# Pairs of images in the front of a deformable-convolution kernel, and GpSimd on part of the sampling tensors

## The chip, the cores and the metric

The kernel runs on one core of a Trainium2 chip. The metric is the device time of one execution in microseconds. The engines of the core run side by side and meet only at semaphores: TensorE (PE; its weight loads are PEld), VectorE (DVE), ScalarE (ACT), GpSimd (POOL) and SyncE (SP), which here only issues transfers. Each engine takes its own instructions in the order in which they are written.

## What is computed

The input x has 4 images of 64 channels and 16 x 16 pixels. Two blocks follow each other, cut here to what matters:

```
x = x + dcn(norm_over_channels(x))
    om      = conv3x3(x, w_off) + b_off          # 27 channels: 9 y offsets, 9 x offsets, 9 masks
    ys, xs  = pixel + tap + offset               # fractional places, one for each of 9 taps
    sampled = bilinear(x, ys, xs) * sigmoid(mask)
    out     = sum over taps and channels of sampled * w_dcn
t = t + moe(norm_over_channels(t))               # tokens = 1024 pixels, 64 channels
    the two best of 8 experts, softmax of the two logits
    out     = sum over experts of weight * (gelu(t W1 + b1) W2 + b2)
```

## The kernel before

**Sampling as a product.** A bilinear sample is a sum over all 256 source pixels with the weight hat(ys - y) * hat(xs - x), where hat(d) = max(0, 1 - |d|). The kernel makes this matrix of weights for each tap (256 source by 256 target pixels) and multiplies the image by it on TensorE. The matrix is made in two ways. Images 0 and 1 are DIRECT: the hats of the y and of the x axis are made with the target pixel on the partition, 16 numbers each, and a product of the two, repeated along the two axes (`pr`, line 589, 512 columns for a chunk of two taps and half of the pixels), gives the transposed matrix; TensorE transposes it (T steps, line 861), ScalarE or VectorE copies it out of PSUM (E steps, lines 480 and 739), and M steps (line 875) multiply the image. Images 2 and 3 are SPREAD: their hats are made with (tap, place) on the partition (`hrow`, and `hlast` for the ninth tap), written to a tensor in DRAM, and read back so that they lie spread over the source pixels (30 reads of SyncE, lines 332 and 335); a product (`pd`, line 600) gives the matrix with no transpose.

**The front, step by step.** For each image: `stats`, `rstd` (a power on GpSimd, line 349) and `xn` (line 699) normalize; `xnT` transposes; `xpl` (ScalarE) and `xpu` (VectorE, line 705) write two halves of a padded image; `conv` (line 830) makes the 27 offset channels in four column groups of 32 partitions, each a partial sum; `om` copies them. DIRECT: `omT` transposes and sums the groups, `pos`, `dist` (line 566), `abs` (ScalarE), `relu` (line 724), `haty` (line 577) make the hats, then 10 products `pr` for each image, written as pr image.chunk.half. SPREAD: R steps (lines 848 to 852) pick the rows by a matmul with a 0/1 matrix, whose last rows add the place constants, and ScalarE takes absolute values or the tanh of the mask; `hr` steps of VectorE (lines 609 to 618) finish. The constants of the R steps are rows made by GpSimd on one partition (`make_rows`) and brought to their places by seven small transfers of SyncE (lines 310 to 317).

**The rest.** C steps (line 886) project by `w_dcn`; `xr` adds; `oT`, `st`, `rstdt`, `lna`, `xT`, `xs` normalize again; gate, `top`, `idx`, `wd` choose experts for a half (two images) at a time; H (line 937), Gelu (`g`, line 511), O (line 948), `tmp` (line 770) are the experts, `ya` (GpSimd, line 416) and F add them up.

**The order** of each engine is a list of steps written out by hand at lines 44 to 67, and HOMES and PAIR_HOMES give each step its PSUM bank. A step waits only for the semaphores of what it reads and of what it overwrites. The products write to a ring of AT_RING = 3 chunks, so chunk u waits until chunk u - 3 is transposed.

Of the kernel before, what the change touches and what calls it, by code (L numbers as in the profile page):

```python
# [33 lines left out]
DIRECT, SPREAD = (0, 1), (2, 3)  # L34
# [5 lines left out]
POS_ROW = 3 * OMG + OM  # L40
LESS = 2 * HW
BIG = LESS + 3 * TAPS * W

PE_ORDER = (
    "xnT0 early4 conv0 xnT2 xnT3 omT0 xnT1 conv2 conv3 conv1 R2.0 R2.1 R3.1 T0.0 T0.2 T0.3 R3.0 T0.1 T0.4 omT1 T0.5 T0.8 T0.7 "
    "T0.6 M0.0 M0.4 M0.1 M0.3 M0.2 T1.0 T1.1 T1.3 T1.5 T1.2 T1.4 T1.7 T1.6 T1.8 M1.0 M1.3 M1.2 M1.4 M1.1 C0.0 C1.0 C0.1 C1.1 M2.2 "
    "oT1 oT0 M2.0 M2.3 M2.1 M2.4 xT0 xT1 C2.0 M3.0 M3.1 C2.1 gate0 H0.2.0 H0.0.0 H0.1.1 H0.1.0 H0.0.1 H0.2.1 oT2 M3.3 M3.2 wdT0 "
    "M3.4 C3.0 O0.1 C3.1 sp0.0 sp0.1 H0.3.0 oT3 O0.0 O0.2 xT2 xT3 H0.3.1 gate1 H1.0.0 H1.0.1 H1.1.0 H1.1.1 H1.2.1 wdT1 O0.3 O1.0 "
    "sp1.0 sp1.1 H1.3.1 H1.2.0 H1.3.0 O1.1 O1.2 O1.3.0 F0 O1.3.1 Fa1.0 Fa1.1 F1.0 F1.1 "
).split()  # L50
ACT_ORDER = (
    "xpl0 om0 xpl2 xpl3 xpl1 tanhm0 abs0 om2 selr0 om3 ay2 al2 tm2 tl2 om1 E0.0 tm3 E0.3 ay3 E0.1 E0.2 tanhm1 E0.5 abs1 E0.7 E0.6 "
    "se0.0 al3 E0.4 se0.3 E1.0 E1.1 tl3 E1.5 E1.2 se0.1 E1.7 E1.4 E1.8 se1.2 se0.4 se1.1 se1.3 se2.2 se2.3 se2.1 xs1 xs0 se2.4 "
    "g0.2.0.1 tanhd0 se3.1 g0.0.0.0 g0.2.0.0 g0.0.0.1 g0.1.0.0 g0.1.0.1 g0.1.1.0 g0.1.1.1 g0.2.1.0 se3.3 g0.0.1.1 g0.0.1.0 se3.4 "
    "wts0 g0.2.1.1 ss0.1 g0.3.0.1 g0.3.0.0 xs2 xs3 g0.3.1.1 g0.3.1.0 g1.0.0.1 g1.0.0.0 g1.0.1.1 tanhd1 g1.0.1.0 g1.1.1.0 g1.1.0.1 "
    "g1.1.0.0 g1.1.1.1 g1.2.1.1 wts1 g1.2.1.0 ss1.0 ss1.1 g1.2.0.0 g1.2.0.1 g1.3.1.0 g1.3.0.0 g1.3.0.1 g1.3.1.1 "
).split()
DVE_ORDER = (
    "stats0 stats1 xn0 base0 xpu0 xn2 xn3 xn1 xpu2 xpu3 pos0 dist0 xpu1 relu0 haty0 pr0.1.0 pr0.0.0 pr0.0.1 pr0.1.1 hr2.0 hr2.1 "
    "hr2.2 pr0.2.0 pr0.2.1 pr0.4.0 pr0.4.1 pr0.3.0 pr0.3.1 pos1 dist1 E0.8 relu1 haty1 pr1.2.1 pr1.0.0 pr1.0.1 pr1.1.0 hr3.0 "  # L60
# [19 lines left out]
        "conv2 R2.0 T0.0 T0.1 T0.8 M0.4 C0.0 oT0 M3.4 O0.1 F0 Fa1.1 "  # L80
    ),
    (
        "T0.2 T0.7 M0.1 M1.0 M1.4 M2.0 xT2 O1.1 "
    ),
    (
        "R3.0 T0.5 M0.0 M0.3 T1.0 T1.2 T1.8 xT3 "
# [929 lines left out]
```

## Time and profile before

| | us |
|---|---|
| median of 3 runs | 90.9 (90.84 to 90.98) |
| the profiled execution | 90.21 |
| its span, first to last instruction | 88.4 |
| TensorE busy | 80.9 |
| VectorE busy | 64.5 |
| ScalarE busy | 46.9 |
| GpSimd busy | 20.6 |

The span leaves out 1.8 us around it. A row of a timeline gives start, length, engine, line, operation, output and inputs with their sizes, and in brackets how long the engine stood idle before it and who released it. One matrix product in float32 is two matmul instructions. In a row of several instructions the length runs from the first start to the last end. Lengths on GpSimd are rough.

### The profile page before, as it was taken

What the parts mean: (1) busy time and instruction counts of PE and PEld (TensorE: products, weight loads), DVE (VectorE), ACT (ScalarE), POOL (GpSimd) and SP (SyncE); (2) the same over time, 40 slices, a digit from 0 to 9 for tenths busy, and PEclk for the clock granted to TensorE, in tenths of its full rate; (3) what the DMA queues carried; (4) which work ended last, traced back from release to release, by engine and by line L of the source; (5) the groups of instructions that cost most, each with busy time, mean ns of one, the idle gap of its engine ahead of it and who ended that gap; (6) DMA issues with size and microseconds to landing.
All of it is one profiled execution on the core that took longest, in us unless ns stands there. A gap on an engine that the chain in (4) does not pass through costs nothing.

```text
span 88.4 us, 1853 instructions
## 1 busy us (share of the span) xinstructions
PE 80.9 (92%) x606; PEld 48.7 (55%) x606; DVE 64.5 (73%) x199; ACT 46.9 (53%) x95; POOL 20.6 (23%) x39
## 2 busy tenths in 40 slices
PE   3986799999999999969969999999999999999970
PEld 3974455499657968846646535734345332433540
DVE  5999989998999999999954998519667613213470
ACT  4110565787956843211410899814439986889000
POOL 7499820000003040005000002200309103200720
DMA  1520049340999997089999500000000000000012
GB/s 32 160 61 2 2 77 399 129 124 15 293 259 319 296 314 259 1 222 272 311 320 320 164 4 0 7 0 0 0 0 0 0 0 0 0 7 0 0 59 59
DMA packets 7192, 9.92 MB, mean 112 GB/s; under 512 B 1690, under 2 KB 3648, under 8 KB 7184
## 3 DMA queue, kind: packets, MB, share of 16 engines
q1 hardware_dynamic: 6848, 9.42, 35.9%
q0 software_dynamic: 192, 0.30, 1.0%
q8 instruction: 5, 0.08, 0.4%
q10 hardware_dynamic: 144, 0.10, 0.3%
q14 instruction: 3, 0.02, 0.1%
HBM read 8.95 MB, written 0.85 MB: 111 GB/s over the span
## 4 chain that ended last, share of the span: by engine, by line
PE 56%; DVE 19%; DMA 11%; issue 5%; SPq 3%; ACT 1%; POOL 1%; DVEq 0%
PE banks L937 17%; PE banks L948 15%; DMA hat_rows<-hlast 6%; DMA spread_hats<-hat_rows 6%; PE banks L861 5%; DVE front L589 4%; PE banks L875 4%; PE banks L830 3%; DVE xn L699 2%; PE banks L848 2%; SPq L335 2%; PE banks L928 1%; PE banks L886 1%; DVE spread_hats L600 1%; PE banks L919 1%
## 5 line engine op out<-in xcount | busy, mean ns | idle before, releaser
L511 ACT ACTIVATE front<-banks,b_col 128x512 f32<-128x512 f32 x32 | 19.8, 700 | 8.7 <-PE banks L937 5.4
L937 PE MATMUL banks<-x2s,w_sb 64*128 64x512 f32 x64 | 15.2, 608 | 0.0
L948 PE MATMUL banks<-front,w_sb 128*64 128x512 f32 (+1 forms) x72 | 14.7, 549 | 0.0
L770 DVE SCALAR_TENSOR_TENSOR spread_hats<-banks,b_col,spread 128x512 f32<-128x512 f32 (+1 forms) x9 | 6.1, 689 | 9.9 <-PE banks L948 7.3
L349 POOL TENSOR_TENSOR rs<-ve,power 128x2 f32<-128x2 f32 (+1 forms) x6 | 5.2, 868 | 28.7 <-DVE ve L639 27.5
L589 DVE TENSOR_TENSOR front<-hats 128x512 f32<-128x512 f32 (+1 forms) x20 | 11.5, 630 | 0.5 <-PE banks L861 0.3
L600 DVE TENSOR_TENSOR spread_hats<-spread_hats 128x1024 f32<-128x1024 f32 (+1 forms) x10 | 10.8, 1107 | 0.7 <-DMA spread_hats<-hat_rows 0.6
L483 ACT ACTIVATE smp<-banks 128x256 f32<-128x256 f32 x14 | 5.2, 389 | 9.5 <-PE banks L875 9.5
L875 PE MATMUL banks<-spread_hats,xn 128*64 128x256 f32 x72 | 9.0, 384 | 0.7 <-DVE spread_hats L600 0.7
L937 PEld LDWEIGHTS banks<-x2s,w_sb 64*128 64x128 f32 x64 | 5.7, 186 | 6.4 <-issue 2.5
L948 PEld LDWEIGHTS banks<-front,w_sb 128*64 128x64 f32 x72 | 4.9, 137 | 7.8 <-issue 6.2
L861 PE MATMUL banks<-ident,front 128*128 128x128 f32 x72 | 9.1, 277 | 0.1
L480 ACT ACTIVATE front<-banks 128x512 f32<-128x512 f32 x15 | 8.2, 592 | 1.7 <-PE banks L861 1.7
L861 PEld LDWEIGHTS banks<-ident,front 128*128 128x128 f32 x72 | 7.9, 142 | 1.4 <-DVE front L589 0.5
L875 PE MATMUL banks<-front,xn 128*64 128x256 f32 x72 | 8.3, 383 | 0.0
L875 PEld LDWEIGHTS banks<-spread_hats,xn 128*64 128x64 f32 x72 | 4.8, 136 | 3.2 <-issue 1.1
L875 PEld LDWEIGHTS banks<-front,xn 128*64 128x64 f32 x72 | 5.1, 136 | 2.6 <-ACT front L480 0.6
L802 PE MATMUL banks<-ident 128*128 128x128 f32 x26 | 5.1, 374 | 1.4 <-POOL power L356 1.4
L289 POOL DMA_DIRECT2D hat_rows<-hrow x2 | 1.4, 708 | 18.5 <-DVE hrow L609 15.8
L802 PEld LDWEIGHTS banks<-ident 128*128 128x128 f32 x26 | 4.8, 286 | 1.4 <-POOL power L356 1.4
L886 PE MATMUL banks<-smp,wdcn 128*64 128x128 f32 x80 | 5.5, 275 | 0.1
L886 PEld LDWEIGHTS banks<-smp,wdcn 128*64 128x64 f32 x80 | 4.7, 137 | 1.3 <-issue 0.7
(117 smaller groups left out, 102.0 us busy)
## 6 DMA issues: line engine op xcount, KB each, us to landing
spread_hats<-hat_rows SPq DMA_DIRECT2D x24, 256.0 KB, 5.0
w_sb<-in_w SPq DMA_DIRECT2D x2, 512.0 KB, 4.6
spread_hats<-hat_rows SPq DMA_DIRECT2D x6, 128.0 KB, 5.6
xc<-in_x_ch SPq DMA_DIRECT2D x1, 256.0 KB, 5.5
hat_rows<-hrow SPq DMA_DIRECT2D x2, 128.0 KB
hat_rows<-hrow POOLq DMA_DIRECT2D x2, 128.0 KB, 5.5
xt<-in_x_tok SPq DMA_DIRECT2D x1, 192.0 KB, 2.5
wdcn<-in_w_dcn SPq DMA_DIRECT2D x1, 160.0 KB, 2.9
```

The costliest lines, as they stand in the source:

```text
L349: pool.tensor_tensor(dst, src, power[:, 0:src.shape[1]], ALU.pow).then_inc(ready, 1)
L480: act.activation(a_sb[:, k, :, :].rearrange("p s t -> p (s t)"), bank(f"T{d}.{k}"), ACT.Copy).then_inc(tap_saved["ACT"], 1)
L511: act.activation(hid[:, m % H_RING, half, c, :], two_banks(f"H{h}.{j}.{c}")[:, half * 512:(half + 1) * 512], ACT.Gelu, bias=b1_col[:, col: ...
L589: dve.tensor_tensor(at[:, u % AT_RING, j, 0:m, :].rearrange("p k (y x) -> p k y x", x=W), hats[:, i, j, k0:k0 + m, :].unsqueeze(3).broadca ...
L600: dve.tensor_tensor(spread_hats[:, i, 1:, k0:k0 + m, :], spread_hats[:, i, 1:, k0:k0 + m, :], spread_hats[:, i, 0, k0:k0 + m, :].unsqueeze ...
L770: dve.scalar_tensor_tensor(part(tmp[:, h, j, :]), part(bank(step_o)[:, :]), b2_col[:, j:j + 1], part(spread[:, h, j, :]), ALU.add, ALU.mul ...
L802: pe.matmul(home[:, 0:P], ident[:, :], ident[:, :], start=True, stop=True)
L861: last = pe.transpose(bank(step)[:, st * HW + j * P:st * HW + (j + 1) * P], at[:, u % AT_RING, j, place, st * P:(st + 1) * P], ident[:, :])
L875: last = pe.matmul(bank(step)[col * C:(col + 1) * C, 0:HW], xn[:, NT * b + st, 0, :], tap(b, k, st), start=(st == 0 or len(taps) == 1), st ...
L886: last = pe.matmul(bank(f"C{b}.0")[j * O:(j + 1) * O, 0:P], wdcn[:, q, :], smp[:, b, q, j * P:(j + 1) * P], start=(q == 0), stop=(q == CHU ...
L937: last = pe.matmul(two_banks(step)[:, half * 512:(half + 1) * 512], w1_sb[rows_, j, c * P:(c + 1) * P], x2s[rows_, 2 * h:2 * h + 2, :], st ...
L948: last = pe.matmul(part(bank(step)[O * half:O * half + O, :]), w2_sb[:, j + PAIRS * half, c, :], part(hid[:, (PAIRS * h + j) % H_RING, hal ...
```

## The change

DIRECT and SPREAD stay as they are. What changes:

- **Pairs in the front.** `xnT`, `xpl`, `xpu`, `conv` and `om` take two images at once: images 0 and 1, then 2 and 3. A pair's convolution uses the four column groups as two images by two partial sums. `omT`, `pos` and `tanhm` come once, for both DIRECT images. The first transfer of `xt` brings four tiles instead of two. `xpu1` is ScalarE's, `om1` is VectorE's.
- **Row products.** R1.2 (the last tap of both images), R1.0 and R1.1, in which a product uses only one image's 64 rows. Seven products where there were eight. The pixel places are added by `om1`, from a tensor `pos_rows` that GpSimd makes (`make_places`), and the tap's shift is a bias of ScalarE's absolute value (`make_shifts` on GpSimd). `hat_of` is 512 wide, `place_of` (512 wide) is new, `pick` is made in four steps instead of one. `make_rows` and its seven transfers are gone, `hlast` holds both images. All writes of hat rows are SyncE's, both images' ahead of the first reads.
- **GpSimd** makes `dist1`, nine of the twenty `pr` products (seven of 512 columns, two of 256) and `pd2.0` and `pd2.3` of the ten spread products. `sel0` comes later.
- `relu1` moves to ScalarE, `xs2` to VectorE, `ss0.0` to ScalarE, and E and se steps are shared out anew. All orders and bank homes are new.

```diff
 POOL_ORDER = (
-    "rstd0 rows0 rstd1 sel0 dw3 rstdt0 rstdt1 rstdt2 rstdt3 ya0.1 ya0.2 ya0.3 ya1.1 ya1.2 "
+    "rstd0 rstd1 place0 shift0 dist1 pr0.1.1 pr0.2.1 pr0.4.0 pr0.3.1 pr1.0.0 pr1.1.1 pr1.2.1 pr1.3.1 pr1.4.0 pd2.0 pd2.3 rstdt0 "
+    "rstdt1 sel0 rstdt2 rstdt3 ya0.1 ya0.2 ya0.3 ya1.1 ya1.2 "
 ).split()
 PE_ORDER = (
-    "xnT0 early4 conv0 xnT2 xnT3 omT0 xnT1 conv2 conv3 conv1 R2.0 R2.1 R3.1 T0.0 T0.2 T0.3 R3.0 T0.1 T0.4 omT1 T0.5 T0.8 T0.7 "
-    "T0.6 M0.0 M0.4 M0.1 M0.3 M0.2 T1.0 T1.1 T1.3 T1.5 T1.2 T1.4 T1.7 T1.6 T1.8 M1.0 M1.3 M1.2 M1.4 M1.1 C0.0 C1.0 C0.1 C1.1 M2.2 "
...
+    "xnT0 early4 xnT1 conv0 omT0 conv1 R1.2 R1.0 R1.1 T0.2 T0.3 T0.0 T0.1 T0.4 T0.5 M0.0 T0.6 T0.7 T0.8 M0.1 M0.2 M0.3 T1.0 T1.1 "
+    "T1.5 T1.3 T1.2 T1.4 T1.7 T1.6 T1.8 M0.4 M1.2 M1.0 M1.1 M1.3 C0.0 M1.4 C0.1 C1.0 oT0 C1.1 M2.0 oT1 M2.2 M2.1 M2.3 M2.4 xT0 "
...
 DVE_ORDER = (
-    "stats0 stats1 xn0 base0 xpu0 xn2 xn3 xn1 xpu2 xpu3 pos0 dist0 xpu1 relu0 haty0 pr0.1.0 pr0.0.0 pr0.0.1 pr0.1.1 hr2.0 hr2.1 "
-    "hr2.2 pr0.2.0 pr0.2.1 pr0.4.0 pr0.4.1 pr0.3.0 pr0.3.1 pos1 dist1 E0.8 relu1 haty1 pr1.2.1 pr1.0.0 pr1.0.1 pr1.1.0 hr3.0 "
-    "pr1.1.1 pr1.2.0 pr1.3.0 pr1.3.1 pr1.4.1 pr1.4.0 hr3.1 hr3.2 E1.6 E1.3 se0.2 se1.0 pd2.0 pd2.2 se1.4 pd2.1 pd2.3 xr0 xr1 "
...
+    "stats0 stats1 xn0 xn1 xn3 xn2 xpu0 base0 pos0 dist0 om1 relu0 haty0 pr0.0.0 pr0.1.0 pr0.0.1 hy2 hx2 pr0.2.0 hm2 hl1 hy3 "
+    "pr0.3.0 hx3 hm3 haty1 pr0.4.1 E0.5 pr1.2.0 E0.6 pr1.0.1 pr1.1.0 pr1.3.0 E1.3 pr1.4.1 E1.4 E1.1 se0.4 se1.2 pd2.1 se1.0 E1.8 "
+    "pd2.2 xr0 se1.4 xr1 st0 st1 pd2.4 lna0 lna1 pd3.0 se2.4 xr2 se3.0 top0 st2 pd3.2 pd3.1 pd3.3 se3.2 pd3.4 se3.3 idx0 wd0 xr3 "
...
+        def product(engine, b, q, j):
+            i = DIRECT.index(b)
+            u = CHUNKS * i + q
+            k0, m = chunk_taps(q)[0], len(chunk_taps(q))
+            engine.wait_ge(*saved(haty_ready, f"haty{b}"))
+            if u >= AT_RING:
+                before, chunk = divmod(u - AT_RING, CHUNKS)
+                engine.wait_ge(tap_T, upto(*(f"T{DIRECT[before]}.{k}" for k in chunk_taps(chunk))))
+            shape = [P, m, H, W]
+            engine.tensor_tensor(
+                at[:, u % AT_RING, j, 0:m, :].rearrange("p k (y x) -> p k y x", x=W),
+                hats[:, i, j, k0:k0 + m, :].unsqueeze(3).broadcast_to(shape),
+                hats[:, i, j, TAPS + k0:TAPS + k0 + m, :].unsqueeze(2).broadcast_to(shape),
+                ALU.mult).then_inc(*one_more(at_ready, f"pr{b}.{q}.{j}"))
...
                 elif kind == "conv":
                     take_bank(step, saved(om_saved, f"om{b}"))
...
+                    for t in range(2 * KS):
+                        kx, ky = divmod(t, KS)
+                        for i in range(2):
+                            q = 2 * i + t % 2
+                            last = pe.matmul(bank(step)[q * OMG:(q + 1) * OMG, 0:HW], woff[:, t, :],
+                                             xpad[:, 2 * b + i, ky:ky + H, 2 * kx:2 * kx + W], start=(t < 2), stop=(t >= 2 * KS - 2))
...
+                        for c in ((0, 1) if n[1] == 0 else (2,)):
+                            for i in range(2):
+                                rows_ = slice(i * IMG_ROWS, (i + 1) * IMG_ROWS)
+                                first = i * 512 + c % 2 * HW
+                                last = pe.matmul(two_banks(step)[:, first:first + HW], pick[rows_, c * P:(c + 1) * P], om_sp[rows_, :],
+                                                 start=True, stop=True)
```

## Rows read from the trace of the kernel before

**Rows 1.** The page: busy us, share of the span, and instructions of each engine.

```profile
PE 80.9 (92%) x606; PEld 48.7 (55%) x606; DVE 64.5 (73%) x199; ACT 46.9 (53%) x95; POOL 20.6 (23%) x39
```

**Rows 2.** Busy times by stretch: length, busy of each engine, clock, DMA share.

```profile
17.10:31.00 13.90, 13.84 (x117) 11.37 (x116) 13.09 (x28) 10.63 (x24) 0.91 (x2) 1.00 0.73 209
31.00:37.60 6.60, 6.52 (x80) 5.09 (x80) 6.60 (x10) 2.19 (x6) 1.04 (x2) 1.00 0.61 189
```

**Rows 3.** The timeline of TensorE, 11 to 47 us: start, length, line, operation.

```profile
11.16 2.78 PE L830 MATMUL banks<-xpad,woff 128*32 128x256 f32 x36
...
17.12 1.53 PE L861 MATMUL banks<-ident,front 128*128 128x128 f32 x12
18.49 1.03 PE L848 MATMUL banks<-big 128*128 128x256 f32 x4
...
20.23 0.53 PE L838 MATMUL banks<-omsum,om_sb 128*128 128x32 f32 x4
...
26.53 4.60 PE L861 MATMUL banks<-ident,front 128*128 128x128 f32 x36
31.06 4.16 PE L875 MATMUL banks<-front,xn 128*64 128x256 f32 x36
...
37.50 1.06 PE L875 MATMUL banks<-spread_hats,xn 128*64 128x256 f32 x8
39.24 0.43 PE L895 MATMUL banks<-ident,xc 64*128 64x64 f32 x4 [0.68 <-DVE xc L628]
...
46.18 1.08 PE L875 MATMUL banks<-spread_hats,xn 128*64 128x256 f32 x8 [0.70 <-DVE spread_hats L600]
```

**Rows 4.** The start: GpSimd's line 359, VectorE's timeline and its line 699 (min/median/max).

```profile
L359 POOL IOTA hat_of<- x1: 594/594/594, 1.5 to 1.5; 128x384 f32 x1
...
3.75 0.85 DVE L539 BATCH_NORM_STATS2 st<-xt 128x6 f32<-128x64 f32 x6
...
L699 DVE TENSOR_SCALAR xn<-xt,mv,rs x8: 333/390/722, 5.3 to 9.9; 128x128 f32<-128x128 f32 x8
...
7.46 0.43 DVE L705 COPY xpad<-banks 64x256 f32<-64x256 f32 x1
```

**Rows 5.** The timeline of VectorE, 11 to 44 us.

```profile
11.34 0.85 DVE L566 TENSOR_TENSOR dist<-pos,grid 128x576 f32<-128x576 f32 x1
...
23.21 0.46 DVE L724 TENSOR_SCALAR hats<-dist 128x576 f32<-128x576 f32 x1
...
24.20 2.50 DVE L589 TENSOR_TENSOR front<-hats 128x512 f32<-128x512 f32 x4
26.62 0.42 DVE L609 TENSOR_SCALAR hrow<-hrow 128x512 f32<-128x512 f32 x1
...
42.96 1.21 DVE L600 TENSOR_TENSOR spread_hats<-spread_hats 128x1024 f32<-128x1024 f32 x1
```

**Rows 6.** GpSimd and VectorE at once: lines 349, 660 (ns, min/median/max) and both timelines.

```profile
L349 POOL TENSOR_TENSOR rs<-ve,power x6: 696/713/1322, 4.0 to 62.0; 128x2 f32<-128x2 f32 x5, 128x6 f32<-128x6 f32 x1
L660 DVE CAST topf<-topi x2: 171/494/816, 49.9 to 68.1; 128x8 f32<-128x8 uint32 x2
...
54.69 1.07 POOL L349 TENSOR_TENSOR rs<-ve,power 128x2 f32<-128x2 f32 x1 [12.47 <-DVE ve L639]
54.52 0.68 DVE L600 TENSOR_TENSOR spread_hats<-spread_hats 128x512 f32<-128x512 f32 x1
...
67.62 1.26 POOL L416 TENSOR_TENSOR ya<-ya,spread_hats 128x512 f32<-128x512 f32 x1
68.10 0.82 DVE L660 CAST topf<-topi 128x8 f32<-128x8 uint32 x1
```

**Rows 7.** SyncE's queue: the first and the last issues of image 2's 15 reads.

```profile
20.66 0.62 SPq L332 DMA_DIRECT2D spread_hats<-hat_rows  x1
...
29.03 1.32 SPq L335 DMA_DIRECT2D spread_hats<-hat_rows  x2
```

**Rows 8.** The page: DMA issues with KB each and us to landing.

```profile
spread_hats<-hat_rows SPq DMA_DIRECT2D x24, 256.0 KB, 5.0
```

## What the change will do: the prediction

> **What bounds the kernel now.** I read the page first: TensorE is busy for 80.9 of 88.4 us, VectorE for 64.5, GpSimd for 20.6 [rows 1]. Then the busy times by stage: from 17.1 to 31.0 TensorE is busy 13.84 of 13.90 us and VectorE 13.09, and from 31.0 to 37.6 they are busy 6.52 and all 6.60 of 6.60 us [rows 2]. So the front has two bounds that touch: TensorE never rests, and VectorE, which makes what TensorE transposes, hardly does. GpSimd is free there. The clock of TensorE is granted in full in all of it. Then TensorE's timeline [rows 3]: the offset convolutions and the row products (R steps) lie ahead of the first transposes (T steps) at 17.12, the last T step ends at 26.53 + 4.60 = 31.13, and later there are two pauses, 0.68 us for VectorE's add and 0.70 us for a spread product. I take two marks from this, **the start of the T steps (17.12)** and **their end (31.13)**. What comes behind the second mark is TensorE work in a fixed order that the change leaves nearly as it is.
>
> **What the pairs take from TensorE.** Three images' convolutions take 2.78 us [rows 3], 6 waves of four column groups with the second half empty, so 0.46 each; a pair of images fills 3 waves where two images took 4, so two waves (0.9 us) fall away. R steps: R3.0, two products of 256 columns (4 matmul instructions), takes 1.03 us [rows 3]; four such steps, 8 products, are about 4.1 us. After: one product, and 6 that lie on half of the rows each, two at a time, 4 waves of about 0.5 us. That takes 2.1 us away, or 0.5 if halves don't run together. The omT steps become one, 0.36 us less (estimate from 0.53 for 4 matmuls [rows 3]). Only what now lies inside 17.12 to 31.13 counts: R3.0 and omT1, about 0.9 + 0.36 = 1.25 us; the rest empties time in which TensorE will wait for the first products anyhow. Against it, one tap product, M0.4, moves behind the last T step: 0.46 us, a ninth of 4.16 [rows 3].
>
> **What it does to the start.** GpSimd makes more index tensors, 384 wide ones for 0.59 [rows 4], so VectorE gets the fourth at about 3.2 and needs 1.3 for the four steps on `pick` and 0.35 for zeroing the padding: 4.85. Four tiles of statistics, from 0.85 us for six and as much again with their aggregates: 1.0, 5.85. The power of four columns, between 0.70 (two) and 1.32 (six) [rows 4, 6]: 1.0, 6.85. Four xn tiles at 0.35 [rows 4]: 8.25; two images more, which stand ahead of the copy, 1.4, and the copy of a pair 0.7 (0.43 was one image [rows 4]): 10.4. conv0 3 waves: 11.85; its copy, omT0 and `pos`: 12.85; `dist0` 0.8 [rows 5]: 13.65; its absolute value on ScalarE 0.7; `relu0` 0.46 [rows 5]: **14.9**, and without anything in the way products would begin at 15.4, against 13.93 before. Bounds: 14.0 if the index tensors hide, 16 if `xn` is slowed by GpSimd's place tensors, as tiles now range from 333 to 722 ns [rows 4]. The constant rows no longer go through seven small DMAs on SyncE's queue, so the weights are issued some 4 us earlier; nobody waited for them.
>
> **What it moves from VectorE to GpSimd,** the step that decides. A two-input operation of 512 columns takes GpSimd 1.26 us [rows 6] and VectorE 2.50 / 4 = 0.62 [rows 5]. Until the last T step GpSimd has `dist1` (576 columns, 1.4), 7 products of 512 (8.9) and 2 of 256 (about 0.65 each, 1.3): 11.6 us. VectorE keeps 9 products (5.6), 2 halves (0.7), two `haty` (0.9, each taken as a `relu`, 0.46), four row clips at 0.28 (half of the columns of a step of 0.42, with its fixed part; 1.1), two masks of rows (0.7) and the last row (0.7, both estimates from the same 0.42): 9.7 us [rows 5]. If both ran side by side, this would be over in 11.6 us.
>
> Do they? The only rows in which they meet say no. The cast of the indices takes 171 ns alone and 816 ns beside a GpSimd sum: it begins at 68.10 and ends at 68.92, when the sum (67.62 + 1.26 = 68.88) does [rows 6]. A power takes GpSimd about 0.70 us, and 1.07 when it starts at 54.69, under a spread product of VectorE that ends at 55.20: it ends 0.56 us behind that [rows 6]. In both, the later one waits for the earlier, and only its start-up (0.1 us on VectorE, 0.14 on GpSimd) is hidden. Products and `hats` steps on VectorE have their inputs in SBUF, as this spread product has; copies out of PSUM (E, se) have not. I take it that the two streams go **one behind the other**: 9.7 + 11.6 = 21.3 us, less the hidden start-ups, 0.14 for ten GpSimd operations and 0.07 for some ten of VectorE, 2.1 us: 19.2. From 14.9 that ends at 34.1; the last T step, half a microsecond, at 34.6. Nothing is left idle for it to hide in: no GpSimd product can start on image 1 before `haty1`, and VectorE reaches that only behind the rows.
>
> The Trainium skill speaks of this case (SBUF — State Buffer, "Who interferes with whom"): a VectorE instruction with two SBUF inputs and a GpSimd instruction that reads SBUF exclude each other, the second blocking fully until the first is done. The trace agrees in the two meetings above. By its rule with nothing hidden the streams would take the whole 21.3 us, and the forecast would be 2.1 us higher.
>
> **The sum,** against the profiled execution (span 88.4 us, 90.21 in all, so 1.8 around it, and 0.7 under the median 90.9): T steps end 34.6 - 31.13 = +3.5; M0.4 behind them +0.5; of the two pauses of 1.4 us half goes (products are on GpSimd's account there, and image 3's rows are read at once behind image 2's) -0.7; `fin0` no longer stands ahead of the last products, -0.2, and ScalarE instead of VectorE copies `ss0.0`, +0.2; small waits from the new orders in the second half +0.2, an estimate. +3.5: **94.4** for the median 90.9 (a span of about 92).
>
> Covers that I count on: the 30 reads of spread hats now follow each other without a stop, 19.4 us of SyncE's queue (image 2's 15 take 20.66 to 30.35 [rows 7]). With the masks and `hlast` done near 27 and their writes issued by 28, they end near 47.5, and the last lands 5.0 us later [rows 8], near 52.5; its product ran at 54.52 before [rows 6] and is wanted near 58 then. If the cover is gone, each microsecond of it is one. `pd2.0` and `pd2.3` on GpSimd cost 2.4 us each (the double of 1.21 [rows 5]); they follow its last product at 34.1 and are there at about 37 and 40.5 (between VectorE's `pd2.1` and `pd2.2`). TensorE needs 6.4 us of its own between its last T step and the first spread samples, as now (31.13 to 37.50 [rows 3]): they are wanted near 41.5 and 43, and behind them waits the first `rstdt`, which the layer norm needs at about 43.5. That cover is thin: 1 to 2 us.
>
> **Rivals.**
> A, the forecast: one behind the other with start-ups hidden, 94.4 (93 to 95.8). Chance 0.48.
> B, the same, dearer: nothing hidden (+2.1, 96.5), or GpSimd's products cost more than its plain sum, as their inputs are repeated along two axes and the sum's are not (a fifth more on 9 of them is 2 us), or `rstdt` comes late: 95.8 to 98.5. For it: `xn` tiles of up to 722 ns beside GpSimd. Chance 0.24.
> C, on the other side: the two engines run side by side, since only the cast's kind of operation excludes GpSimd. The place that decides is the first pair of products. GpSimd has `dist1` until 16.35, then `pr0.1.1` until 17.65: T steps begin at 17.7 (+0.6). From there TensorE is fed (VectorE and GpSimd make a chunk in 1.3 us, TensorE uses it in 1.9) and has 1.25 less: -0.65 at the second mark with M0.4 inside this sum, and both pauses go, -1.4: -2.0, 88.9 (88.2 to 90.6). It decides from the point at which overlap recovers over 3.5 us of the 9.7. For it: `pr` is not the cast; against it the power beside the spread product. Chance 0.21.
> D: exclusion is real but TensorE's order fills the holes with M steps, 90.7 to 93. Chance 0.07, mostly slower.
>
> **How the numbers follow.** The likeliest gives 94.4. The range of 80% spans C's middle to B's: 88.8 to 97.8. 0.2% (about 0.2 us) is about what a measurement of this kernel can tell from no change. Faster: C but for its edge, 0.20; within: 0.03; slower: A, B and most of D, 0.77.
>
> **What would show it.** In A, VectorE's products beside GpSimd's take 1.2 to 1.9 us each, GpSimd's more than 1.3, their ends alternating; TensorE is idle 4 to 6 us between its first T step and about 35, its transposes waiting for `front`; the last T step ends at 34 to 36. In C VectorE's products stay at 0.68 and the last T step ends before 31. Convolutions of a pair near 1.4 us and four R waves near 2 show the first part. I am wrong in mechanism if products keep their lengths, and wrong in size if the start-ups hide more, if the first product doesn't begin near 17, or if a wait behind 38 (for `pd2.0`, `pd2.3`, `rstdt0`) becomes the longest.

## The result, and the profile after

The changed kernel takes **94.8 us** (94.56 to 96.03 in 4 executions); the kernel before took 90.87 beside it (90.23 to 90.98). The ratio is 1.044, interval 1.038 to 1.050. The profiled execution took 94.73 with a span of 92.9 us, 4.5 more than the 88.4 of before. In what follows, a ratio is that of each kernel's fast executions, those within 1.5% of its fastest, while a median is of all of them, and of "pairs only", "late start" and "no products" the profiled execution was a slow one, so that little behind the T steps is read from it.

The page of after, then its busy times in one stretch (length, busy of TensorE, its weight loads, VectorE, ScalarE and GpSimd with instructions, TensorE's granted clock, DMA share, GB/s):

```profile
PE 81.3 (88%) x600; PEld 49.1 (53%) x600; DVE 61.1 (66%) x193; ACT 45.3 (49%) x87; POOL 45.1 (49%) x60
...
PEclk9997599996599999999999999999999999999999
...
L381 POOL TENSOR_TENSOR front<-hats 128x512 f32<-128x512 f32 (+1 forms) x9 | 12.8, 1435 | 4.4 <-PE banks L944 4.4
...
L381 DVE TENSOR_TENSOR front<-hats 128x512 f32<-128x512 f32 (+1 forms) x11 | 10.6, 982 | 3.0 <-PE banks L944 3.0
```

```profile
19.00:31.00 12.00, 9.32 (x63) 7.18 (x65) 9.89 (x18) 7.34 (x18) 9.57 (x7) 0.86 0.38 116
```

GpSimd's busy time doubled and more (20.6 to 45.1), VectorE's fell only by 3.4, and TensorE has as much to do as before, 81.3 us [rows 1]. Where TensorE had no idle time [rows 2], it is idle for 2.7 of 12 us. And the clock line shows something that the forecast doesn't have: it falls twice, in the slices from 7 to 11.6 and from 21 to 25.5 us.

TensorE's timeline of after (start, length, line, operation, count, idle time ahead and what ended it):

```profile
7.94 1.20 PE L896 MATMUL banks<-ident,xn 128*128 128x128 f32 x4 [2.70 <-DVE xn L765]
8.93 1.91 PE L877 MATMUL banks<-ident 128*128 128x128 f32 x8
10.64 1.02 PE L896 MATMUL banks<-ident,xn 128*128 128x128 f32 x4
11.59 1.50 PE L908 MATMUL banks<-xpad,woff 128*32 128x256 f32 x24
...
16.45 0.67 PE L924 MATMUL banks<-om_sp,pick 128*128 128x256 f32 x2 [0.70 <-DVE om_sp L776]
17.05 1.57 PE L934 MATMUL banks<-om_sp,pick 64*128 64x256 f32 x12
20.62 4.71 PE L944 MATMUL banks<-ident,front 128*128 128x128 f32 x24 [2.00 <-DVE front L381]
...
27.19 1.50 PE L944 MATMUL banks<-ident,front 128*128 128x128 f32 x12 [0.84 <-POOL front L381]
...
31.77 4.45 PE L944 MATMUL banks<-ident,front 128*128 128x128 f32 x36
...
50.99 1.11 PE L1020 MATMUL banks<-x2s,w_sb 64*128 64x512 f32 x4
```

L944 is the line of the T steps. They begin at 20.62 instead of 17.12 and end at 31.77 + 4.45 = **36.22** instead of 31.13 [rows 3]: +5.1. The first 24 of them take 4.71 us, 0.196 each, where the last 36 take 0.124 each. From the second mark to the end of the span it is 56.7 us, against 57.3. So the loss lies wholly ahead of the second mark; behind it the change wins 0.6. The two pauses of before, 0.68 and 0.70 us [rows 3], are gone.

VectorE's timeline of after:

```profile
14.35 0.27 DVE L785 TENSOR_TENSOR pos<-banks,base 128x108 f32<-128x108 f32 x1 [2.05 <-PE banks L916]
14.66 0.76 DVE L360 TENSOR_TENSOR dist<-pos,grid 128x576 f32<-128x576 f32 x1
...
16.22 0.45 DVE L790 TENSOR_SCALAR hats<-dist 128x576 f32<-128x576 f32 x1
16.70 0.46 DVE L369 SCALAR_TENSOR_TENSOR hats<-tanh_m,hats 128x288 f32<-128x288 f32 x1
17.20 1.54 DVE L381 TENSOR_TENSOR front<-hats 128x512 f32<-128x512 f32 x1
18.66 1.54 DVE L381 TENSOR_TENSOR front<-hats 128x512 f32<-128x512 f32 x1
```

And GpSimd's:

```profile
18.14 1.50 POOL L381 TENSOR_TENSOR front<-hats 128x512 f32<-128x512 f32 x1
19.61 1.50 POOL L381 TENSOR_TENSOR front<-hats 128x512 f32<-128x512 f32 x1
...
23.83 3.21 POOL L381 TENSOR_TENSOR front<-hats 128x512 f32<-128x512 f32 x1 [1.28 <-PE banks L944]
...
28.40 1.06 POOL L381 TENSOR_TENSOR front<-hats 128x512 f32<-128x512 f32 x1 [0.34 <-PE banks L944]
...
35.30 2.36 POOL L391 TENSOR_TENSOR spread_hats<-spread_hats 128x1024 f32<-128x1024 f32 x1
```

While both engines make products, one of VectorE's begins every 1.46 us (17.20, 18.66) and one of GpSimd's every 1.47 (18.14, 19.61). Alone, GpSimd's takes 1.06 and VectorE's 0.62 [rows 5]: 1.68 for one behind the other, 0.2 hidden. That is the forecast's picture, but it doesn't fill the stretch: of VectorE's nine products of 512 columns only four take over 1.2 us, and by the page's lines of the products (L381) GpSimd's wait 4.4 us for transposes and VectorE's 3.0, since a product needs a free place in the ring. The product at 23.83 is a case of its own: 3.21 us, during which VectorE ran one step behind another, and it ended only when VectorE had turned to a copy out of PSUM.

### The profile page after: what moved, and what is told of

It reads as the page before. It is cut to its first block, busy times and chain, and to the rows that moved or that the text cites. A ratio compares the mean times of both kernels' runs of the same rounds, so it can differ in the third digit from the quotient of the medians.

```text
span 92.9 us, 1837 instructions
## 1 busy us (share of the span) xinstructions
PE 81.3 (88%) x600; PEld 49.1 (53%) x600; DVE 61.1 (66%) x193; ACT 45.3 (49%) x87; POOL 45.1 (49%) x60
## 4 chain that ended last, share of the span: by engine, by line
PE 76%; DVE 10%; POOL 7%; issue 3%; ACT 0%; POOLq 0%; DVEq 0%
PE banks L1020 16%; PE banks L1031 15%; PE banks L958 15%; PE banks L944 10%; PE banks L969 5%; POOL front L381 3%; DVE front L381 3%; PE banks L908 3%; PE banks L896 2%; PE banks L877 2%; PE banks L1011 1%; PE banks L984 1%; PE banks L1002 1%; POOL rs L416 1%; PE banks L994 1%
## 5 line engine op out<-in xcount | busy, mean ns | idle before, releaser
L381 POOL TENSOR_TENSOR front<-hats 128x512 f32<-128x512 f32 (+1 forms) x9 | 12.8, 1435 | 4.4 <-PE banks L944 4.4
L416 POOL TENSOR_TENSOR rs<-ve,power 128x2 f32<-128x2 f32 (+1 forms) x6 | 6.2, 1036 | 17.9 <-DVE ve L709 15.1
L1031 PE MATMUL banks<-front,w_sb 128*64 128x512 f32 (+1 forms) x72 | 14.8, 550 | 0.0
L944 PE MATMUL banks<-ident,front 128*128 128x128 f32 x72 | 10.6, 308 | 3.0 <-DVE front L381 2.0
L381 DVE TENSOR_TENSOR front<-hats 128x512 f32<-128x512 f32 (+1 forms) x11 | 10.6, 982 | 3.0 <-PE banks L944 3.0
L944 PEld LDWEIGHTS banks<-ident,front 128*128 128x128 f32 x72 | 9.3, 159 | 4.7 <-issue 4.0
L600 ACT ACTIVATE front<-banks 128x512 f32<-128x512 f32 x12 | 6.6, 599 | 5.8 <-PE banks L944 5.8
L391 DVE TENSOR_TENSOR spread_hats<-spread_hats 128x1024 f32<-128x1024 f32 (+1 forms) x8 | 9.0, 1141 | 0.0
L603 ACT ACTIVATE smp<-banks 128x256 f32<-128x256 f32 x12 | 4.2, 386 | 9.7 <-PE banks L958 9.7
L517 POOL TENSOR_TENSOR ya<-ya,spread_hats 128x512 f32<-128x512 f32 x3 | 3.8, 1269 | 7.6 <-DVE spread_hats L845 7.4
L391 POOL TENSOR_TENSOR spread_hats<-spread_hats 128x1024 f32<-128x1024 f32 x2 | 5.1, 2540 | 3.2 <-DMA spread_hats<-hat_rows 3.2
L517 POOL TENSOR_TENSOR ya<-spread_hats 128x512 f32<-128x512 f32 x2 | 2.5, 1272 | 7.6 <-DVE spread_hats L845 7.6
```

The source lines that it names most:

```text
L381: engine.tensor_tensor(at[:, u % AT_RING, j, 0:m, :].rearrange("p k (y x) -> p k y x", x=W), hats[:, i, j, k0:k0 + m, :].unsqueeze(3).broa ...
L391: engine.tensor_tensor(spread_hats[:, i, 1:, k0:k0 + m, :], spread_hats[:, i, 1:, k0:k0 + m, :], spread_hats[:, i, 0, k0:k0 + m, :].unsque ...
L416: pool.tensor_tensor(dst, src, power[:, 0:src.shape[1]], ALU.pow).then_inc(ready, 1)
L517: pool.tensor_tensor(ya[:, h, :], so_far, tmp[:, h, j, :], ALU.add).then_inc(ya_ready, 1)
L600: act.activation(a_sb[:, k, :, :].rearrange("p s t -> p (s t)"), bank(f"T{d}.{k}"), ACT.Copy).then_inc(tap_saved["ACT"], 1)
L944: last = pe.transpose(bank(step)[:, st * HW + j * P:st * HW + (j + 1) * P], at[:, u % AT_RING, j, place, st * P:(st + 1) * P], ident[:, :])
```

## The experiments

The forecast stands, but a sum can be right by luck. Two causes can be told apart, since each can be had alone: **the pairs** and **GpSimd's share**. "The pairs" stands here for all of the change but GpSimd's share, with the row products and the moved steps; these weren't separated further. One measure serves in all runs: the time at which the first product begins, and the end of the T steps. The table collects them from the timelines of VectorE and TensorE (profiled executions), with the median time and its ratio to the kernel before on the same chip.

| kernel | first product | T steps begin | T steps end | end less first product | median us | ratio (interval) |
|---|---|---|---|---|---|---|
| before | 13.93 | 17.12 | 31.13 | 17.2 | 90.87 | 1 |
| after | 17.20 | 20.62 | 36.22 | 19.0 | 94.8 | 1.044 (1.038 to 1.050) |
| pairs only | 18.40 | 19.84 | 35.78 | 17.4 | 95.76 | 1.053 (1.040 to 1.065) |
| GpSimd only | 14.01 | 17.77 | 33.18 | 19.2 | 93.29 | 1.028 (1.018 to 1.038) |
| after, warm | 16.20 | 19.59 | 33.99 | 17.8 | 93.85 | 1.030 (1.015 to 1.046) |
| pairs only, warm | 16.18 | 19.42 | 33.58 | 17.4 | 94.20 | 1.038 (1.028 to 1.048) |
| middle filler | 18.45 | 21.71 | 36.11 | 17.7 | 94.80 | 1.040 (1.030 to 1.051) |
| early start | 16.00 | 20.22 | 33.83 | 17.8 | 93.72 | 1.034 (1.028 to 1.040) |
| rows first | 16.00 | 19.31 | 33.77 | 17.8 | 93.59 | 1.029 (1.018 to 1.040) |
| distances only | 16.00 | 19.10 | 33.53 | 17.5 | 94.26 | 1.035 (1.024 to 1.046) |
| late start | 16.82 | 18.87 | 33.62 | 16.8 | 96.12 (lowest 94.08) | – |

The fifth column is what the study came to. With pairs it is 17.4 to 17.8, whoever makes the products and whatever the orders are, but for after itself (19.0, with slow transposes in it).

The lines behind the first and third columns, of before, of "pairs only, warm" and of "late start":

```profile
13.93 2.50 DVE L589 TENSOR_TENSOR front<-hats 128x512 f32<-128x512 f32 x4
```

```profile
30.29 3.29 PE L944 MATMUL banks<-ident,front 128*128 128x128 f32 x28 [0.30 <-DVE front L381]
```

```profile
16.82 2.50 DVE L590 TENSOR_TENSOR front<-hats 128x512 f32<-128x512 f32 x4
...
29.02 4.60 PE L866 MATMUL banks<-ident,front 128*128 128x128 f32 x36
```

**Pairs only.** After, with `dist1`, all products and all spread products back on VectorE; ScalarE takes image 1's absolute value later, as `dist1` comes later.

```diff
-    "rstd0 rstd1 place0 shift0 dist1 pr0.1.1 pr0.2.1 pr0.4.0 pr0.3.1 pr1.0.0 pr1.1.1 pr1.2.1 pr1.3.1 pr1.4.0 pd2.0 pd2.3 rstdt0 "
-    "rstdt1 sel0 rstdt2 rstdt3 ya0.1 ya0.2 ya0.3 ya1.1 ya1.2 "
+    "rstd0 rstd1 place0 shift0 rstdt0 rstdt1 sel0 rstdt2 rstdt3 ya0.1 ya0.2 ya0.3 ya1.1 ya1.2 "
```

> The changed kernel with dist1, the nine products and pd2.0 and pd2.3 back on VectorE (abs1 and relu1 stand later on ScalarE so that nothing blocks); all else of the change stays. Theory 1 (VectorE's two-input operations and GpSimd's exclude each other, so GpSimd takes more from the front than it gives): products on VectorE back at 0.68 us each, last transposes end near 33 instead of 36.2, 90 to 92 us. Theory 2 (the pairs are what costs, GpSimd helps): VectorE has 9 more products and is later, 96 us or more.

Measured 95.76, above theory 1 and just below theory 2. If GpSimd's share were the cause, this would have been the good kernel; it is no better than after. Its products take 0.68 us as expected, but the T steps end at 35.78, not near 33. TensorE shows why the first product comes as late as 18.40: the 24 convolution instructions of the first pair need 2.65 us, where the next 24 need 1.50.

```profile
7.93 1.20 PE L896 MATMUL banks<-ident,xn 128*128 128x128 f32 x4 [2.29 <-DVE xn L765]
...
11.62 2.65 PE L908 MATMUL banks<-xpad,woff 128*32 128x256 f32 x24
...
15.44 1.50 PE L908 MATMUL banks<-xpad,woff 128*32 128x256 f32 x24
```

**GpSimd only.** The kernel before with the same steps on GpSimd (`dist1`, nine products, two spread products). GpSimd now comes late to image 3's rows, so SyncE writes them.

```diff
-    "rstd0 rows0 rstd1 sel0 dw3 rstdt0 rstdt1 rstdt2 rstdt3 ya0.1 ya0.2 ya0.3 ya1.1 ya1.2 "
+    "rstd0 rows0 rstd1 sel0 pr0.1.1 pr0.2.1 pr0.4.0 pr0.3.1 dist1 pr1.0.0 pr1.1.1 pr1.2.1 pr1.3.1 pr1.4.0 pd2.0 pd2.3 rstdt0 "
+    "rstdt1 rstdt2 rstdt3 ya0.1 ya0.2 ya0.3 ya1.1 ya1.2 "
```

> The kernel before with GpSimd alone: it makes dist1, the same nine products, pd2.0 and pd2.3, and SyncE writes image 3's hat rows in its place; no pairs. Theory 1: VectorE's products take 1.0 to 1.5 us beside GpSimd's, TensorE idles 2 us or more before 35, 93 to 96 us. Theory 2 (side by side): products stay at 0.68 us and the time is 89 to 91 us.

Measured 93.29, ratio 1.028, so some 2.5 us over the before of its chip. Here GpSimd's share does cost: the T steps start 0.65 late, with a pause of 0.50 for a product, and end 2.05 late, at 30.02 + 3.16 = 33.18; behind them stands a second price. GpSimd's spread product (start 31.87, 2.53 us) holds VectorE's small mask step, and TensorE waits for the copy behind that:

```profile
32.12 2.57 DVE L621 SCALAR_TENSOR_TENSOR hrow<-mrow,hrow 128x256 f32<-128x256 f32 x1
```

```profile
36.08 3.24 PE L883 MATMUL banks<-front,xn 128*64 128x256 f32 x28 [1.88 <-DVE front L747]
```

The same step for the other image took 0.43 in this trace. In the changed kernel the row masks stand ahead of GpSimd's last products, and none meets `pd2.0`.

**After, warm, and pairs only, warm.** Both get more filler for TensorE: 18 in place of 9 transposes of the identity before the first `xn`, and eight more groups of two ahead of the T steps. No result depends on them; what they change is that TensorE isn't idle there.

```diff
-WARM = 9
+WARM = 18
...
-    "xnT0 early4 xnT1 conv0 omT0 conv1 R1.2 R1.0 R1.1 T0.2 T0.3 T0.0 T0.1 T0.4 T0.5 M0.0 T0.6 T0.7 T0.8 M0.1 M0.2 M0.3 T1.0 T1.1 "
+    "xnT0 early4 xnT1 conv0 omT0 conv1 R1.2 R1.0 R1.1 early8 T0.2 T0.3 T0.0 T0.1 T0.4 T0.5 M0.0 T0.6 T0.7 T0.8 M0.1 M0.2 M0.3 "
```

> The changed kernel with dummy matmuls in its two early pauses of TensorE: 18 instead of 9 at the very start, and 8 between R1.1 and T0.2. Theory 3 (the lower clock of the transposes after the pause of 2 us is on the path, since both engines wait for transposes to free the ring): granted clock 1.00 throughout, transposes at 0.13 us an instruction, 1.5 to 2.5 us less, 92.3 to 93.3 us. Theory 4 (the products set the pace, the clock is beside it): the clock comes back and the time stays within 0.5 us of 94.8.

> Pairs without GpSimd, and with the dummy matmuls. Theory 1 with theory 3: 88.5 to 90.5 us, faster than both kernels. Theory 1 alone: as the kernel with pairs only. Theory 2: 95 us.

Measured 93.85 (93.76, 93.94, 93.23 and 95.19) and 94.20 (94.19 to 94.22); after gains 1.0 us by the fillers, where theory 3 had 1.5 to 2.5. TensorE's timeline of "after, warm":

```profile
9.78 0.66 PE L896 MATMUL banks<-ident,xn 128*128 128x128 f32 x4
10.59 1.50 PE L908 MATMUL banks<-xpad,woff 128*32 128x256 f32 x24 [0.16 <-DVE xpad L771]
...
29.54 4.45 PE L944 MATMUL banks<-ident,front 128*128 128x128 f32 x36
```

VectorE's products in it (count, min/median/max in ns, start of the first and of the last):

```profile
L381 DVE TENSOR_TENSOR front<-hats x11: 414/693/1680, 16.2 to 32.1; 128x512 f32<-128x512 f32 x9, 128x256 f32<-128x256 f32 x2
```

and the same row of "pairs only, warm":

```profile
L381 DVE TENSOR_TENSOR front<-hats x20: 411/684/693, 16.2 to 32.3; 128x512 f32<-128x512 f32 x16, 128x256 f32<-128x256 f32 x4
```

What was slow is at full rate: the pair's convolution begins at 10.59, and the T steps behind it take 0.13 each. That is worth 2.2 us at the T steps' end (36.22 to 33.99), but 1.0 in the whole time. And of two kernels that differ in GpSimd's share alone, the one makes all 20 at 0.68 us on VectorE, starting them from 16.2 to 32.3; the other makes 11 there and 9 on GpSimd, and VectorE starts its own from 16.2 to 32.1. GpSimd's help and its disturbance cancel. Busy times of "after, warm", then of "pairs only, warm", from the first product on:

```profile
16.20:34.00 17.80, 16.38 (x134) 12.73 (x136) 17.10 (x25) 10.34 (x24) 13.18 (x12) 1.00 0.41 122
```

```profile
16.20:34.00 17.80, 16.43 (x138) 13.05 (x140) 17.49 (x35) 10.87 (x25) 0.00 (x0) 1.00 0.63 187
```

VectorE, the third busy time, hardly rests in either (17.10 and 17.49 of 17.80 us; the first has its waits for GpSimd inside). It is what this stretch goes by, so a late first product moves the end of the T steps with it. That "pairs only, warm" would reach 88.5 to 90.5 was wrong.

Where the other 1.2 us went, the stretch behind the T steps tells. In "after, warm" SyncE's first read of spread hats is issued at 26.91, in after at 26.88: the rows didn't get earlier with the T steps, since VectorE writes them between products that stand beside GpSimd's. So two spread products now wait for data, and TensorE for VectorE behind them. VectorE's timeline, then TensorE's:

```profile
36.47 1.23 DVE L391 TENSOR_TENSOR spread_hats<-spread_hats 128x1024 f32<-128x1024 f32 x1 [0.56 <-DMA spread_hats<-hat_rows]
...
39.37 1.23 DVE L391 TENSOR_TENSOR spread_hats<-spread_hats 128x1024 f32<-128x1024 f32 x1 [0.75 <-DMA spread_hats<-hat_rows]
```

```profile
41.24 0.30 PE L978 MATMUL banks<-ident,xc 64*128 64x64 f32 x2 [0.73 <-DVE xc L698]
...
46.97 0.41 PE L984 MATMUL banks<-ident,xn 128*128 128x128 f32 x2 [0.25 <-DVE xn L822]
...
48.56 1.08 PE L958 MATMUL banks<-spread_hats,xn 128*64 128x256 f32 x8 [0.16 <-DVE spread_hats L391]
```

From the T steps' end to the first expert product it is 16.3 us here and 14.8 in after, and 1.1 of the 1.5 are these three waits. In "pairs only, warm" the reads begin at 23.48 and the spread products don't wait for them; there TensorE waits 0.36 and 0.39 for VectorE, which has more to do.

**Beside reading, beside writing.** The disputed mechanism by itself: eight unused operations of 512 columns on GpSimd, in the kernel before, from the moment at which image 0's products begin. Once they read SBUF and once they only write.

```diff
+                elif kind == "load":
+                    pool.wait_ge(haty_ready, 1)
+                    for n_ in range(8):
+                        pool.tensor_tensor(scr[:, n_, :, :], ident[:, :].unsqueeze(1).broadcast_to([P, 4, P]),
+                                           ident[:, :].unsqueeze(1).broadcast_to([P, 4, P]), ALU.mult)
```

```diff
+                        pool.memset(scr[:, n_, :, :], 0.0)
```

> The kernel before with 8 products of 128x512 on GpSimd, which read SBUF and whose results nobody uses, released when haty0 is done; nothing waits for them but the hat rows of image 3, long after. Theory 1 (two-input VectorE operations and reading GpSimd operations exclude each other): VectorE's products beside them take 1.2 to 1.7 us and the time grows by 4 us or more. Rival (only copies and clips of VectorE are excluded): products stay at 0.68 us and the time grows by less than 1 us.

> The kernel before with 8 fills of 128x512 on GpSimd in the same place, which read nothing. If it is GpSimd's reading that excludes a two-input operation: products stay at 0.68 us, time within 0.5 us of before. If any GpSimd operation excludes: products beside them take 1 us or more, and 1.5 us or more are lost.

Reading, 96.55 us, ratio 1.064 (1.055 to 1.073), two executions; in the profiled one TensorE's clock falls too, behind a pause of 3.48 us, and has a part in the size. VectorE's products:

```profile
13.94 0.69 DVE L595 TENSOR_TENSOR front<-hats 128x512 f32<-128x512 f32 x1
14.55 1.53 DVE L595 TENSOR_TENSOR front<-hats 128x512 f32<-128x512 f32 x1
16.00 1.52 DVE L595 TENSOR_TENSOR front<-hats 128x512 f32<-128x512 f32 x1
```

and GpSimd's:

```profile
15.50 1.48 POOL L421 TENSOR_TENSOR scr<-ident 128x512 f32<-128x512 f32 x1
...
23.23 4.30 POOL L421 TENSOR_TENSOR scr<-ident 128x512 f32<-128x512 f32 x1
```

Writing, 92.51 us, ratio 1.019 (1.011 to 1.027). VectorE's rows:

```profile
15.77 0.69 DVE L594 TENSOR_TENSOR front<-hats 128x512 f32<-128x512 f32 x1
16.37 1.68 DVE L614 TENSOR_SCALAR hrow<-hrow 128x512 f32<-128x512 f32 x1
```

The two runs say it without any other change. Beside a reading GpSimd, products take 1.52; beside a writing one, 0.68. The last GpSimd operation, begun ahead of six products of VectorE that take 0.67 (512 columns) or 0.41 (256) each, takes 4.30 us. The writing run missed its time (+1.6 instead of under 0.5): the row clip, one input and one output in SBUF, takes 1.68 instead of 0.42 and ends just behind the fills. So that kind is held by writes as well, and the T steps end at 32.00. A pause of 1.90 before a spread product, where before has 0.70, makes up the rest. The Trainium skill draws the line in the same place (SBUF — State Buffer, "Who interferes with whom"): an instruction of VectorE with two SBUF inputs contends with a GpSimd instruction that reads SBUF, one in a two-port mode with any. By that rule the clip would be of the second sort (alone it takes 0.42 us, where a product of as many columns takes 0.68), and both runs agree.

**Late start.** The kernel before with five unused VectorE products ahead of `haty0`, nothing else; the first product moves from 13.93 to 16.82.

```diff
+                elif kind == "late":
+                    for n_ in range(b):
+                        dve.tensor_tensor(scr[:, n_, :, :], ident[:, :].unsqueeze(1).broadcast_to([P, 4, P]),
+                                          ident[:, :].unsqueeze(1).broadcast_to([P, 4, P]), ALU.mult)
```

> The kernel before with 5 products nobody uses on VectorE ahead of haty0, 3.1 us, so that the first product comes near 17.0, as late as in the changed kernel; nothing else differs. Theory 5 (the late start alone makes the loss of the pairs): last transposes near 34.2 and 3 us more, 93.5 to 94.2 us. Theory 6: VectorE has slack behind and gives it back, 92 us or less.

94.08 us is the lowest of its four executions, 3.2 over the 90.92 beside it, for products that begin 2.9 late; the others took 96.11 (the profiled one), 96.13 and 97.90. Of the 2.9 us 2.5 arrive at the end of the T steps, so hardly any of it is absorbed. What it costs in all isn't settled: in the profiled execution a spread product then waits 2.38 us for its data, and TensorE pauses for 2.44 where before has 0.70. 3.2 is the least.

**Middle filler.** After with the middle one of the two fillers alone (the longer row of `early8` above, WARM left at 9).

> The changed kernel with only the 8 dummy matmuls between R1.1 and the first transposes. Theory 3 (the pause of 2.0 us there lowers the clock of the transposes): transposes at 0.13 us an instruction, last one ends near 34.5 instead of 36.2, and most of the gain of both fillers, 93.7 to 94.2 us. Rival (the early pause matters, conv0 late): 94.6 us or more.

```profile
11.62 2.72 PE L908 MATMUL banks<-xpad,woff 128*32 128x256 f32 x24
...
21.71 1.07 PE L944 MATMUL banks<-ident,front 128*128 128x128 f32 x8
```

Measured 94.80, the time of after, where theory 3 had 93.7 to 94.2. The transposes now take 0.134 each, but the pair's convolution 2.72, and the first product comes at 18.45. What the transposes win (end less first product 17.7 instead of 19.0) the start loses (+1.25). The filler can't have slowed the convolution, as it stands behind it and the program is that of after up to there; "pairs only" has the same slow convolution. So why the slow stretch at the start is longer in these two traces than in after's isn't known. With both fillers, the eight filler instructions, both groups of `xn` transposes and the convolution run at full rate. The early filler alone wasn't run; that it is the one that counts is argued from these rows.

**Early start and rows first.** Both try to bring the first product forward, on top of "after, warm". The first puts the pair's convolution ahead of the second group of transposes, with two filler groups ahead of it instead of four, `om0` ahead of `xpu1` and `xpl1` on ScalarE, `xpu0` ahead of `xn2` and `om1` behind `haty0` on VectorE. The second also moves the row values ahead of image 1's absolute value (`abs1`) on ScalarE, which had waited 3.02 us for GpSimd's `dist1` and held the rows behind it, and has three filler groups instead of eight ahead of the T steps.

```diff
-    "xnT0 early4 xnT1 conv0 omT0 conv1 R1.2 R1.0 R1.1 T0.2 ...
+    "xnT0 early2 conv0 xnT1 omT0 conv1 R1.2 R1.0 R1.1 early8 T0.2 ...
...
-    "stats0 stats1 xn0 xn1 xn3 xn2 xpu0 base0 pos0 dist0 om1 relu0 haty0 pr0.0.0 ...
+    "stats0 stats1 xn0 xn1 xn3 xpu0 xn2 base0 pos0 dist0 relu0 haty0 om1 pr0.0.0 ...
```

```diff
-    "xpl0 xpu1 xpl1 om0 abs0 tanhm0 abs1 al1 tl2 tl3 ay2 tm2 ax2 ax3 tm3 ay3 E0.0 E0.1 relu1 E0.2 ...
+    "xpl0 om0 xpu1 xpl1 abs0 tanhm0 al1 tl2 tl3 ay2 tm2 ax2 ax3 tm3 ay3 abs1 E0.0 E0.1 relu1 E0.2 ...
```

> The changed kernel with GpSimd's share as it is, the dummy matmuls of the run before, and the head of the orders mended: conv0 stands ahead of xnT1 on TensorE with 4 dummy instructions instead of 8 ahead of it, its copy ahead of xpu1 and xpl1 on ScalarE, one xn image instead of two ahead of xpu0, and om1 behind haty0 instead of ahead of relu0 on VectorE. Theory 5 (the late first product, 17.2 against 13.9, is what the pairs cost): first product at 15.0 to 15.7, 1.5 to 2.2 us less than with the dummy matmuls alone, 91.7 to 92.4 us. Theory 6 (the front is bound behind the first product, by the excluded streams): 93.4 us or more.

> The kernel with the early start, with two more edits: ScalarE makes the row values (al1 to ay3) ahead of abs1, which waits 3.0 us for GpSimd's dist1 in that run, and only 3 dummy matmuls instead of 8 stand ahead of the first transposes, where 8 ended at 20.38, behind the first products (19.2). Theory 7 (VectorE reaches pr0.3.0 and haty1 late because the row values come late): row steps start near 18.8 instead of 20.1, the last transposes end near 33.0 instead of 33.8, 92.7 to 93.1 us. Theory 6 (the excluded streams bind whatever the order): within 0.3 us of 93.7.

93.72 and 93.59: both stay with theory 6, and neither reached what it was built for. The first product comes at 16.00, not at 15.0 to 15.7, 0.20 earlier than in "after, warm", and the T steps end 0.16 and 0.22 earlier, not near 33.0. The convolution does start 0.53 earlier (10.06), but pair 1's copy `om1`, 0.48 us, which lay in the wait for ScalarE before, now stands between `haty0` and the first product. The order of the rows made no difference to the end of the T steps (33.83, 33.77), but of the two waits for data that "after, warm" has, rows first has one, of 0.29.

**Distances only.** Rows first, with all products and spread products on VectorE; GpSimd keeps `dist1` alone. One copy goes to ScalarE.

```diff
-    "rstd0 rstd1 place0 shift0 dist1 pr0.1.1 pr0.2.1 pr0.4.0 pr0.3.1 pr1.0.0 pr1.1.1 pr1.2.1 pr1.3.1 pr1.4.0 pd2.0 pd2.3 rstdt0 "
-    "rstdt1 sel0 rstdt2 rstdt3 ya0.1 ya0.2 ya0.3 ya1.1 ya1.2 "
+    "rstd0 rstd1 place0 shift0 dist1 rstdt0 rstdt1 sel0 rstdt2 rstdt3 ya0.1 ya0.2 ya0.3 ya1.1 ya1.2 "
```

> The kernel with rows first, with all products (nine pr, pd2.0, pd2.3) back on VectorE and only dist1 on GpSimd; E0.6 moves to ScalarE. Theory 6: GpSimd's products give about as much as they take, so the last transposes end within 0.7 us of the run with them, 92.3 to 93.8 us; but the first transposes come at 17.4 instead of 19.2, since VectorE makes the first two products in 1.2 us and waits for nobody. Theory 2 (GpSimd's help is needed): 95 us or more.

94.26 (94.18 to 94.27), against 93.59 (93.03 to 93.86) for rows first on the same chip: without GpSimd's products it is 0.7 slower, neither the 92.3 to 93.8 of theory 6 nor the 95 of theory 2. In the profiled executions the T steps end 0.24 earlier, but the stretch behind them is 58.8 us instead of 57.4; the two spread products are VectorE's again there. So the share for GpSimd costs a little ahead of the second mark and wins more behind it.

**No products.** The kernel before with `dist1`, `pd2.0` and `pd2.3` on GpSimd, no product.

```diff
-    "rstd0 rows0 rstd1 sel0 dw3 rstdt0 rstdt1 rstdt2 rstdt3 ya0.1 ya0.2 ya0.3 ya1.1 ya1.2 "
+    "rstd0 rows0 rstd1 sel0 dist1 pd2.0 pd2.3 rstdt0 rstdt1 rstdt2 rstdt3 ya0.1 ya0.2 ya0.3 ya1.1 ya1.2 "
```

> The kernel before with only dist1, pd2.0 and pd2.3 on GpSimd and image 3's hat rows written by SyncE; all pr products stay on VectorE, no pairs. Theory 1: the nine products are what costs in the kernel with GpSimd alone (93.3), so this one is within 0.7 us of before, 90.3 to 91.6 us. Rival (the spread products and the powers queued behind them cost): 92.5 us or more.

92.26, ratio 1.012 (0.997 to 1.028): no difference from before is shown, and neither of the two expectations is met. One of its five executions took 204.48 us; why isn't known. In the profiled one, of 93.95 us, GpSimd reaches `pd2.0` early, in the midst of VectorE's products, and one of these waits for the whole of it; TensorE pauses for 2.30 us, and the 28 transposes behind the pause take 0.18 each:

```profile
26.61 2.37 POOL L384 TENSOR_TENSOR spread_hats<-spread_hats 128x1024 f32<-128x1024 f32 x1 [3.48 <-DMA spread_hats<-hat_rows]
```

```profile
26.68 2.85 DVE L373 TENSOR_TENSOR front<-hats 128x512 f32<-128x512 f32 x1
```

```profile
30.52 5.11 PE L868 MATMUL banks<-ident,front 128*128 128x128 f32 x28 [2.30 <-DVE front L373]
```

## Why the prediction was right, and where it was not

94.4 was said, 94.8 came, with the sign and nearly all of the size. Rival A was to be recognized by products of 1.2 to 1.9 us, ends that alternate, GpSimd's at over 1.3, 4 to 6 us of idle TensorE, and the last T step at 34 to 36. The products held where the engines meet (1.54, and 1.50), but three of VectorE's nine of 512 columns took 0.68 or 0.69, and two of GpSimd's seven 1.06. The idle time between the R steps' end and 35 us is 3.1 (2.00, 0.84, 0.18 and less), with slow matmuls for the rest, and the T steps ended at 36.22, just outside. Step by step:

- **The pairs on TensorE.** Conv of a pair 1.50 us (1.4 said), R steps 0.67 + 1.57 = 2.24 (2.1 said). Right.
- **The start, "relu0 14.9".** Wrong by 1.8: it ends at 16.67, above the upper bound of 16, and the first product begins at 17.20, not at 15.4. (The forecast's last sentence wants a first product near 17, which doesn't fit its own 15.4.) The copy of the pair ended near 10.4, as forecast. But "conv0 3 waves: 11.85" let the convolution start at once. In TensorE's order stand the fillers and the second group of transposes, 1.91 + 1.02 us ahead of it, at half rate: it starts at 11.59 and ends at 13.09 (+1.25). From there to `pos` it was 1.5 us, not 1.0 (+0.5).
- **"One behind the other, 19.2 us".** The exclusion is shown by the reading and the writing run. The length agrees, 19.0 from the first product to the T steps' end where 19.2 was said, but by luck. 1.2 us of it are TensorE's slow transposes; without them it is 17.8. A product costs GpSimd 1.06 alone, not 1.26 (and not more, as rival B had it), and takes longer only where it meets VectorE. And the sum left out VectorE's copies out of PSUM, five of 0.68 us in that stretch, and the waits of both engines for a place in the ring, 3.0 and 4.4 us. Of the two meetings from which it took the rule, only the power beside the spread product has two SBUF inputs on VectorE; the cast has one.
- **What I compared it with.** The step that I called decisive isn't. The sum set the two streams in a row against the two side by side, and never against VectorE doing all of it, 17.4. Against that, GpSimd's share costs 0.2 to 0.4 at the second mark, but in all it is 0.35 to 0.7 us faster (93.85 against 94.20; 93.59 against 94.26). Only in the kernel before, where products start early and TensorE is kept full, does it cost, some 2.5 us.
- **TensorE's clock.** Not in the forecast. In rows 2 it is granted in full, and 36 transposes take 0.128 each there (4.60 / 36 [rows 3]). After has two slow stretches, one behind a pause of 2.7 us and one behind 2.0; "pairs only" and "middle filler" have theirs behind 2.29, "no products" behind 2.30. Filling both pauses was worth 2.2 us at the second mark, 1.0 in all.
- **Behind the second mark.** M0.4 took its 0.46 there. The pauses gave all of their 1.4, not half. The net was -0.6, where the terms add up to 0.0 (+0.5 - 0.7 - 0.2 + 0.2 + 0.2). The covers held: the reads were issued by 46.7 (47.5 said), `pd2.0` came at 37.7 and `pd2.3` at 43.6, and TensorE didn't stop for any of them.

So +1.6 too little at the second mark, 0.6 too much behind it; the span was +4.5 where +3.5 was said, and the median of before, above its profiled execution, took half of that back. That 94.4 and 94.8 lie so near is in part luck. The sign comes from a reason that the forecast had at half its size (products from 15.4, +1.5): **the pairs make the first product 3.3 us late (2.3 where TensorE isn't slow), and the end of the T steps moves with it.** "Late start" shows it without pairs (2.9 late, 2.5 at the second mark), "pairs only, warm" without GpSimd's share (2.25 late, 2.45 at the second mark). A pair's convolution needs both images in `xpad`, and began at 11.59. In the kernel before image 0 went alone, as this row of TensorE's timeline shows:

```profile
8.04 1.06 PE L830 MATMUL banks<-xpad,woff 128*32 128x256 f32 x12 [0.78 <-DVE xpad L705]
```

What stays open. What an earlier start of the reads alone would give wasn't tried; that they hold "after, warm" is read from its timeline, not from a run. "Pairs only, warm" loses 3.5 us, of which 2.45 stand at the second mark and 0.46 are M0.4; the rest isn't traced. Whether "no products" costs anything isn't settled. The two attempts at an earlier first product both stopped at 16.00, so what 15.0 would give isn't known. And which part of the change but GpSimd's share makes the loss is read from the timelines, not from runs. None of these kernels beats the one before.

## What to carry to other kernels

When work is moved to a second engine that can block the first, compare with the first engine doing all of it, not with a free overlap: here the move gave 0.35 to 0.7 us in one kernel and cost some 2.5 in the other. Before that, ask when the first piece comes out: grouping that saves matmuls but delays the first result by 2.25 us cost 2.45 us at the end of the stage, since VectorE was fully loaded all through it. And put long GpSimd operations where VectorE has nothing but copies out of PSUM to do, as one small step of VectorE can wait for the whole of them.

## What the runs showed of the hardware

- Two streams of products, VectorE's and GpSimd's, can alternate strictly: 1.46 us for one of each, 0.2 below the sum of 0.62 and 1.06. But GpSimd can also be shut out for far longer than one instruction, 3.21 and 4.30 us for an operation of 1.06 (after; beside reading). VectorE issues without a gap in both cases; what decides between them isn't shown.
- The reverse is a block of a whole long instruction: 2.57 instead of 0.42 ("GpSimd only"), and 2.85 instead of 0.68 ("no products"), beside a GpSimd operation of 1,024 columns.
- GpSimd's product of two repeated operands takes 1.06 us, less than its plain sum of the same size (1.26 [rows 6]).
- Behind a pause of 2.0 us a transpose takes TensorE 0.196 us on the average of 24, later 0.124: the granted clock of that stretch falls to 0.5, the lower (1.2 GHz) of its two levels, in one slice of it. In "pairs only" and "middle filler" the convolution takes 2.65 and 2.72 instead of 1.50, though the mean granted clock of these executions is 1.00: their records of the clock begin only at 14.0 and 14.1 us, near its end. Durations of like instructions told it here, and the mean did not.
